# An edge-message layer on one core: the transposes of the edge features, the copies behind them and the edge remainders change their places in three engines' orders

## The reference, cut to what matters

```python
h = relu(edge_attr @ W1 + b1)                       # edge_attr (E, 16), W1 (16, 256)
w_edge = (h @ W2 + b2).reshape(-1, 16, 16)          # W2 (256, 256)
msgs = einsum('ei,eio->eo', x[src], w_edge)         # one 16-vector a message
aggr = segment_sum(msgs, dst, num_segments=n_nodes)
out = aggr + x @ root + bias                        # then batch norm and relu
```

## Time and profile before

| | |
|---|---|
| timed runs | 8177.59 us median of 3 (8175.65 to 8178.09) |
| profiled execution, span | 8221.3 us |
| busy, share of the span | PE 89%, PEld 78%, DVE 81%, ACT 54%, POOL 69% |
| first layer | 404 groups, the first gather at 62.03 us |

### The profile page before, as it was taken

One profiled execution on the slowest core, in us unless ns is written; L12 is line 12 of the kernel. 1 busy time (PEld: TensorE's weight loads), 2 busy tenths in 40 slices (PEclk: granted clock), 3 DMA queues, 4 the chain that ended last, 5 costly groups with the idle time before them and its releaser, 6 DMA issues. The chain is left out here.

```text
span 8221.3 us, 191064 instructions
## 1 busy us (share of the span) xinstructions
PE 7349.2 (89%) x52997; PEld 6446.6 (78%) x52997; DVE 6691.0 (81%) x17449; ACT 4457.4 (54%) x8279; POOL 5696.0 (69%) x4866
## 2 busy tenths in 40 slices
PE   7888888888888888888888886999999999999998
PEld 5667676666676666666676765999999999999996
DVE  6777777777777777777777777999999999999997
ACT  3333333333333333333333335888888878778884
POOL 6666666666666666666666664888888888888886
PEclk8999999999999999999999998999999999999999
DMA  2000000000000000000000014444444455554443
GB/s 60 18 17 17 17 17 17 17 17 17 17 17 17 17 18 17 17 17 18 17 17 17 17 23 101 73 75 74 74 75 74 74 73 74 72 74 75 73 75 64
DMA packets 713464, 341.73 MB, mean 42 GB/s; under 512 B 422115, under 2 KB 656599, under 8 KB 713427
## 3 DMA queue, kind: packets, MB, share of 16 engines
q1 hardware_dynamic: 379313, 272.94, 13.1%
q0 software_dynamic: 332928, 64.86, 12.9%
q10 hardware_dynamic: 1186, 3.51, 0.1%
HBM read 307.85 MB, written 32.96 MB: 41 GB/s over the span
## 5 line engine op out<-in xcount | busy, mean ns | idle before, releaser
L802 POOL DMA_INDIRECT xg<-gather_rows,idx x3132 | 3041.9, 971 | 1882.4 <-issue 1848.5
L919 PE MATMUL ps_w<-W2s,hT 128*128 128x256 f32 x12928 | 3240.2, 408 | 37.1 <-issue 36.6
L919 PEld LDWEIGHTS ps_w<-W2s,hT 128*128 128x128 f32 x12928 | 2678.5, 207 | 581.6 <-issue 97.0
L1745 POOL DMA_INDIRECT sums<-total,row x1616 | 2551.0, 1579 | 529.1 <-issue 474.4
L1708 PE MATMUL ps_wide<-hot_col,placed 128*128 128x392 f32 x12928 | 2434.7, 345 | 4.8 <-DVE placed L1544 2.1
L1708 PEld LDWEIGHTS ps_wide<-hot_col,placed 128*128 128x128 f32 x12928 | 2313.6, 196 | 12.2 <-issue 6.9
L841 ACT ACTIVATE hT<-ps_h,b1c 128x512 f32<-128x512 f32 x1616 | 1022.8, 680 | 2302.1 <-PE ps_h L905 2090.8
L1002 DVE TENSOR_TENSOR prod<-ps_w,xg 128x512 f32<-128x512 f32 x1616 | 1098.1, 690 | 969.7 <-remote 599.7
L1544 DVE SCALAR_TENSOR_TENSOR placed<-ps_r,src_r,halves 128x512 fp32r<-128x512 f32 x1616 | 1097.5, 741 | 0.1
L1643 ACT ACTIVATE square<-iota_col,minus_col 128x784 bf16<-128x784 int16 x1212 | 1061.3, 938 | 66.6 <-issue 58.0
L1009 DVE TENSOR_REDUCE msg<-prod 128x32 f32<-128x512 f32 x1616 | 1058.9, 676 | 0.0
(11 more groups left out here) (229 smaller groups left out, 5425.0 us busy)
## 6 DMA issues: line engine op xcount, KB each, us to landing
dst_row<-dst_rows SPq DMA_DIRECT2D x404, 256.0 KB
src_row<-src_rows SPq DMA_DIRECT2D x404, 128.0 KB
xg<-gather_rows,idx POOLq DMA_INDIRECT x3132
q_win<-q_rows SPq DMA_DIRECT2D x404, 96.0 KB
ea<-in_edge_attr SPq DMA_DIRECT2D x404, 64.0 KB
sums<-total,row POOLq DMA_INDIRECT x1616
e<-in_edge_attr SPq DMA_DIRECT2D x404, 32.0 KB
q_rows<-Q SPq DMA_DIRECT2D x12, 768.0 KB, 5.4
```

What stands on the lines that cost most here:

```text
L802: pool.indirect_dma_start(xg[r][:, t, :], None, k.rows, bass.IndirectOffsetOnAxis(ap=idx[r][:, t:t + 1], axis=0)).then_inc(xg_in[r][t], 16)
L919: last = pe.matmul(to, hT[half][:, j, col:col + P], k.W2[:, j, :], start=(j == 0), stop=(j == 1 and not with_b2))
L1745: pool.indirect_dma_start(k.sums[t], bass.IndirectOffsetOnAxis(ap=row[r][:, t:t + 1], axis=0), total[r][:, t, :], None, compute_op=ALU.add ...
```

## The change

Three orders change; no instruction is added, removed or altered.

- PE, body g: `turn(g + 2)` moves from behind `edge_weights` of half 1 to ahead of it (and behind `hidden` of group g + 1).
- ScalarE, body g: the relu of the second half (`relu(g * 2 + 3, 1)`) moves behind `edges_T`, the indices and `edges_hi`; `edges_mid(g + 3)` moves ahead of the two message copies.
- DVE, body g: `edges_res(g + 3)` moves ahead of the last sum and the bias; `edges_lo(g + 3)` moves from behind the low message part to between the first four one-hots and the message remainder.

```diff
@@ scalar, body
                     if ahead or g + 1 < G:
                         relu(g * 2 + 2, 0)
-                        relu(g * 2 + 3, 1)
                     if ahead or g + 2 < G:
                         edges_T(g + 2, s)
                     if ahead or g + AHEAD < G:
                         indices(g + AHEAD, (r + AHEAD) % RING)
                     if ahead or g + 3 < G:
                         edges_hi(g + 3, 1 - s, lap * (RING // 2) + (r + 3) // 2)
+                    if ahead or g + 1 < G:
+                        relu(g * 2 + 3, 1)
+                    if ahead or g + 3 < G:
+                        edges_mid(g + 3)
                     msg_hi(g, s)
                     msg_mid(g, s)
-                    if ahead or g + 3 < G:
-                        edges_mid(g + 3)
@@ tensor, body
                     edge_weights(g * 2, 0, (0, 1))
                     if ahead or g + 1 < G:
                         hidden(g * 2 + 2, g + 1, 0, 1 - s)
-                    edge_weights(g * 2 + 1, 1, (0, 1), dense(r, lap))
                     if ahead or g + 2 < G:
                         turn(g + 2)
+                    edge_weights(g * 2 + 1, 1, (0, 1), dense(r, lap))
@@ vector, body
                     sum_unit(g, s, 2)
+                    if ahead or g + 3 < G:
+                        edges_res(g + 3, 1 - s)
                     sum_unit(g, s, 3)
                     add_bias(g, s, r)
+                    one_hot(g, s, (0, 1, 2, 3))
                     if ahead or g + 3 < G:
-                        edges_res(g + 3, 1 - s)
-                    one_hot(g, s, (0, 1, 2, 3))
+                        edges_lo(g + 3)
                     msg_residue(g, s)
                     one_hot(g, s, (4, 5, 6, 7))
                     msg_lo(g, s)
-                    if ahead or g + 3 < G:
-                        edges_lo(g + 3)
```

## The result

The changed kernel takes 9034.8 us (median of 4, 9024.8 to 9105.5) against 8177.2 us (8175.7 to 8178.1): a ratio of 1.1068, 95% interval 1.1052 to 1.1085. It is **858 us slower**, where 412 us less was forecast, and outside the range (7480 to 8240 us). The profiled execution spans 9042.2 us. Only the first layer changed: in the page's slices the second layer is as before, and begins later.

A forecast was written before the change was run, and what follows sets the result against it. The prediction took a loop of gathers and PE's late signals as the bound; the middle of 10.5 and 11.7 us a group, 11.1, saves 1.02 us x 404 = 412 us: 7765 us, range 7480 to 8240.

The forecast's parts named there:

- What bounds the kernel: First layer: no engine is full; gathers run, PE's late signals follow, the next gathers wait for them; 12.12 us a group.
- the floor of a group: Lower end of the forecast: DVE without its waits for PE, 12.12 - 1.65 = 10.5 us a group.
- PE's part: Transposes ahead of the second sixteen matmuls: their signal 3.4 us earlier, POOL's gap up to 2.2 us a group shorter.
- the late stretch: Time in PE's body when its signals arrive late, read from 2508.6 to 2512.68 us in one body, 4.1 us.
- ScalarE: cost nothing: Second relu behind 1.5 us of other work, covered by 3.4 us of PE's big matmuls, 1.9 us to spare.
- what the turn needs: PE's transposes wait for DVE's last edge part: 1.3 us early in one body read, 0.8 us late in the other.
- The slower rival: PE waits at the transposes for DVE's last part, 0.8 us in every second group: 8340 us, in every group 8500; chance 0.16.
- The late stretch stays: PE's signals stay late equally long wherever the transposes stand: no change, 8178 us, within 16 us; chance 0.12.
- A small gain: Only PE's queue cover grows, easing its stall and slow matmuls: 0.5 us a group down to 0.1, 7975 to 8135 us; chance 0.17.
- freed altogether: DVE also loses 0.5 us of issue at L1002: 10.0 us a group, 7330 us; chance 0.05.
- The rule: PE's stalls would come from instruction fetches at the loop's taken branch, not from the order: time stays at 8178 us.
- What was looked for: Signs if right: L802's idle down over 1 us a group, L919 under 0.24 us busy each, 11.1 us a group.

The follow-up runs named there:

- the run with the middle part first: Changed kernel with ScalarE's middle edge part put ahead of the second relu instead of behind it: 9124.5 us, 1.1102 of the kernel before.
- half trains: Four gathers a group in place of eight, the other tiles zeros: 7268.5 us in the changed kernel, 7428.0 us in the kernel before.
- the two trains in the changed kernel: Changed kernel whose fifth gather of a group also waits for the first unit of TensorE's next body: 8543.9 us, 1.0457 of the kernel before.
- Memsets on GpSimd: Changed kernel with four gathers a group, followed by four memsets of 900 columns on GpSimd in place of the other four: 7536.5 us, ratio 0.9163.

## Why the prediction was wrong, point by point

- **What bounds the kernel: right, and not followed to its end.** The loop was read as it is: a train runs, the held signals come out about 1.7 us after its last gather (the relu 1.66 to 1.80 us after it in four kernels here; in the kernel before, the first at 1.43 us, 2512.60), the next train starts on one of them. Gathers and pause made 12.1 us, and leaving gathers out showed it. But the floor of a group was then taken from VectorE (10.5 us), and POOL's need was put at 9.9 us without the pause. With the pause it is 11.9 to 12.1. Of the 1.02 us a group, no kernel here with the same gathers gained more than 0.1.
- **The step that failed** is in PE's part: "That is ahead of 2508.6, the first signal that I see come late. So the turned signal should fall in front of the late stretch more often than not, POOL finds it when its train ends, and its gap falls from 2.5 to 0.3 us". It took the late stretch to stand at a fixed place of PE's body, while the very signal that starts the train was being moved. The stretch moves with the train. Started earlier, it holds the small matmuls' signal, and behind that stand the relu, the next small matmuls and the transposes themselves. The earlier "turned" never came early: in the round shown the transposes start only after the hold (2521.59), and the gap of POOL rose from 2.5 to 5.5 us.
- **ScalarE: cost nothing, right by itself.** Without PE's part 8187.7 us, 0.15% above the kernel before. The sentence "if the turn's signal comes late, the relu is behind it" looked for the lateness at the wrong signal.
- **VectorE and "what the turn needs": right by itself.** Of the 39.6 us in 3000 that PE idles ahead of the transposes, 23.7 are put down to it, 0.11 us a group. VectorE's 3.6 us of waiting ahead of L990 had no price, as the run with the middle part first showed.
- **The slower rival** (0.16) had the sign and not the mechanism. It priced PE's wait for VectorE at 0.8 us a group, at most 8500 us. The loss came from a loop that the forecast itself had named, run the other way round.
- **"The late stretch stays"** (0.12) held that the stretch has the same length wherever the turn stands. It has not: from the first held signal's matmul to its update 4.1 us in the kernel before (2508.56 to 2512.65) and 6.7 in the changed one (2512.86 to 2519.59). What stays is the distance to the last gather. But its evidence from the earlier trace rows stands: there the gathers follow each other 0.30 us apart from 112.46 on past 131, and the updates of the small matmuls of 121.65 stand at 127.00 and 127.03, in the midst of them. In the changed kernel's steady stretch it is about one in eight: 59 of the 453 small matmuls held for over 0.3 us have their update ahead of the train's end. What lets these out early is open.
- **"A small gain" and "freed altogether"** did not come: the loop through the trains bounded the group, and not VectorE or PE. With half trains the order alone is worth 2.1%, some 160 us, the size of the small gain.
- **The rule weighed.** q8 and q14 moved 15 and 22 packets again, as in the earlier trace rows, with 858 us more in the layer. By the Trainium skill, Runtime: NRT & Kernel Launch, section Instruction fetch mechanics, a taken branch whose target lies outside the two pages in hand has to wait for a DMA fetch. As the cause of these stalls that was rightly put aside: one wait of GpSimd, exchanged, made and unmade the whole loss.
- **What was looked for.** Of the rows named there, three went the wrong way: L802's idle time rose by 2.3 us a group instead of falling by 1, L841's rose by 2.9, and the big matmuls take 0.264 us each (0.250 before), at a mean granted clock of 0.88 instead of 0.93.

## What to carry to other kernels

When a loop goes through a long train of another engine's DMA issues, find out what starts the train before moving that instruction: an earlier start is not a gain by itself, and it moves everything that the train disturbs. Test it with the wait alone; one line of waiting showed here, in both directions, what four engines' worth of reordering had hidden. And put the pause that a loop needs into the floor of the engine that makes it.

## What the runs showed of the hardware

- **Signals of TensorE are held while GpSimd issues indirect gathers back to back** (0.95 us each, 0.30 us between). Free, a relu starts 0.43 us after its pair of matmuls does; in a train of eight it came 6.8 us after. In the rounds read, the hold had begun between 2.9 and 7.4 us after the train's start, at no fixed time. What waits for it restarted 1.26 to 1.80 us after the last gather's end behind seven or eight gathers, and 1.11 to 1.13 us behind four; some signals come out in the midst of a train. VectorE's updates in the same trains stand 0.01 us after its instruction's end. Memsets on GpSimd do not hold TensorE's.
- Which of the gathers' doings holds them (their semaphores, their descriptors, the rows that they move) stays open; neither the size of the rows nor the count of semaphores was varied. Why the middle part first gained nothing stays open too. The 4.6% of the two trains in the changed kernel fits a train of eight at another place (its pauses are 3.10 us in the median, 2.51 in the kernel before), but nothing forecast its size.
- **GpSimd's memsets slow VectorE's one-hots:** 475 ns each beside 281 with the same half trains and no memsets.
- **The granted clock was lower behind PE's waits.** In the changed kernel sixteen big matmuls took 4.88 us at 2507.27, after PE had been busy for 1.66 of the 4.11 us ahead, and 3.62 us at 2513.25, after it had been busy throughout. The mean granted clock was 0.75 from 2507.27 to 2512.10 and 1.00 from 2513.25 to 2516.90; of its two levels, 1.2 and 2.4 GHz, the first stretch had both and the second only the upper. It is 1.00 in the steady stretch with half trains, where such a matmul is busy 0.228 us (2253.1 / 9883).
